# A graph network's relation sum: padding chunks left to GpSimd, the first dense tile transposed in place, and a tile's products put ahead of the next tile's transposes

## What is computed

```
seg = edge_type * n + dst
agg = segment_sum(x[src], seg, num_segments=34 * n)
cnt = segment_sum(ones, seg, num_segments=34 * n)
mean = agg.reshape(34, n, -1) / maximum(cnt, 1.0).reshape(34, n, 1)
h1 = einsum('rni,rio->no', mean, W_rel) + x @ W_root + b_rgcn
xw = h1 @ W_gcn
```

## Time and profile before

| | us |
|---|---|
| median of 3 timed runs | 2950.74 |
| lowest and highest | 2941.15 and 2956.47 |
| profiled execution | 2960.18 |
| its span, first to last instruction | 2958.1 |
| TensorE busy | 2565.2 (87%) |
| VectorE busy | 1549.8 (52%) |
| ScalarE busy | 1133.6 (38%) |
| GpSimd busy | 833.3 (28%) |

### The profile page before, as it was taken

One profiled execution on the slowest core, in us unless ns is written; L12 is line 12 of the kernel. 1 busy time (PEld: TensorE's weight loads), 2 busy tenths in 40 slices (PEclk: granted clock), 3 DMA queues, 4 the chain that ended last, 5 costly groups with the idle time before them and its releaser, 6 DMA issues.

```text
span 2958.1 us, 52403 instructions
## 1 busy us (share of the span) xinstructions
PE 2565.2 (87%) x14479; PEld 2416.0 (82%) x14513; DVE 1549.8 (52%) x2724; ACT 1133.6 (38%) x1977; POOL 833.3 (28%) x1090
## 2 busy tenths in 40 slices
PE   0666779859999999999999999678878889988799
PEld 0244579859999999999999999657778789978799
DVE  7754443463344434433444343488754687687634
ACT  3111242223444444444444444365532246446421
POOL 1677300004555555555555555100000000000000
PEclk9998889989999999999999999899989999989899
DMA  4100011144555555555555554687730200011102
GB/s 166 54 1 1 0 40 38 48 159 165 176 176 187 191 186 177 177 178 172 179 186 191 186 176 144 210 299 252 237 120 33 85 28 10 11 43 54 54 11 95
DMA packets 116745, 361.99 MB, mean 122 GB/s; under 512 B 22254, under 2 KB 22722, under 8 KB 116642
## 3 DMA queue, kind: packets, MB, share of 16 engines
q1 hardware_dynamic: 78241, 224.33, 22.0%
q0 software_dynamic: 38464, 137.17, 13.4%
HBM read 271.90 MB, written 93.37 MB: 123 GB/s over the span
## 4 chain that ended last, share of the span: by engine, by line
PE 77%; DVE 9%; issue 6%; ACT 3%; DMA 3%; DVEq 2%; ACTq 0%; SPq 0%; POOL 0%; POOLq 0%
PE ps L1352 51%; PE ps L1407 12%; PE ps L1343 5%; PE ps L1466 4%; PE ps L1541 3%; DMA land<-messages 1%; DVE h_act L999 1%; ACT land L750 1%; DVE w_a L924 1%; DVE land L1053 1%; DVEq L1184 1%; DMA land<-in_L_gnn_W 1%; ACT agg_w L760 1%; DVE land L1012 0%; DVE xw L1310 0%
## 5 line engine op out<-in xcount | busy, mean ns | idle before, releaser
L1352 PE MATMUL ps<-w_a,h_t 128*128 128x384 f32 x5580 | 1022.1, 339 | 1.9 <-DVE h_t L930 1.5
L1352 PEld LDWEIGHTS ps<-w_a,h_t 128*128 128x128 f32 x5580 | 971.5, 190 | 6.5 <-DVE h_t L930 3.9
L1407 PE MATMUL ps<-xw,agg_w 128*128 128x384 f32 x2800 | 528.6, 351 | 86.4 <-DVE agg_w L1024 55.3
L1407 PEld LDWEIGHTS ps<-xw,agg_w 128*128 128x128 f32 x2800 | 516.6, 198 | 95.3 <-issue 85.4
L1352 PE MATMUL ps<-xw,h_t 128*128 128x384 f32 x3132 | 577.3, 341 | 0.0
L1257 DVE TENSOR_TENSOR h_t<-ps,h_t 128x256 fp32r<-128x256 f32 x516 | 218.4, 423 | 678.4 <-ACT h_t L858 475.0
L1352 PEld LDWEIGHTS ps<-xw,h_t 128*128 128x128 f32 x3132 | 548.9, 188 | 0.0
L858 ACT ACTIVATE h_t<-ps 128x256 fp32r<-128x256 f32 x516 | 198.2, 384 | 669.5 <-PE ps L1352 443.3
L659 POOL DMA_INDIRECT messages<-land,rec_stage x172 | 199.6, 1161 | 353.0 <-ACT land L852 349.6
L1343 PE MATMUL ps<-ident,land 128*128 128x128 f32 x1398 | 196.8, 278 | 91.8 <-DVE land L937 33.3
L1343 PEld LDWEIGHTS ps<-ident,land 128*128 128x128 f32 x1398 | 168.8, 143 | 105.3 <-issue 44.8
(11 more groups left out here) (212 smaller groups left out, 2034.0 us busy)
## 6 DMA issues: line engine op xcount, KB each, us to landing
land<-in_L_gnn_W_rel SPq DMA_DIRECT2D x68, 1152.0 KB
land<-messages SPq DMA_DIRECT2D x92, 768.0 KB, 5.7
land<-x_state SPq DMA_DIRECT2D x40, 384.0 KB, 3.1
land<-in_L_gnn_W SPq DMA_DIRECT2D x10, 1152.0 KB
x_state<-land SPq DMA_DIRECT2D x30, 384.0 KB, 2.3
adj<-x_state SPq DMA_DIRECT2D x10, 384.0 KB, 3.0
h_act<-x_state SPq DMA_DIRECT2D x1, 3840.0 KB
h_table<-h_act SPq DMA_DIRECT2D x10, 384.0 KB, 2.3
```

The source lines that it names most:

```text
L1352: ins = pe.matmul(acc(h), h_t[:, a, k, :], w[:, b, k, h * HF:(h + 1) * HF], start=(k == 0 and a == 0 and b == 0), stop=(stop and k == KB - ...
L1407: ins = pe.matmul(ps[:, 2 + 2 * u + h, 0:wide], agg_w[:, a, b, :], xw[:, c, b, h * HF:h * HF + wide], start=first, stop=last, skip_group_c ...
```

## The change

Three parts. Padding chunks: `ctl_rel[NR]` is now the true number of chunks and `ctl_rel[NR + 1]` the rounded one plus 1. TensorE, VectorE and ScalarE's evacuations run to the true number. GpSimd's loop runs to the rounded number as before, with all its gathers and scatters; for the padding chunks ScalarE only passes its semaphore on, in a small loop (lines of `act.Fori(chunks, filled)`) whose last turn waits for a `ybuf` that GpSimd gives at the stage's end. First dense tile: TensorE transposes `h_act[:, 0]` itself, with no copy and no wait for `x_ring`'s return; VectorE gives `Q.ylow` before it waits for the bias row; it now waits for `R.stored` before it writes `rows[:, 2]`, and for `R.h_back` at the end of a tile's messages. Order: TensorE makes the products of tile t first, then the transposes of tile t + 1.

```diff
@@ GpSimd
-                                (R.wgot[2], 16, 16), (R.wgot[3], 16, 0), (R.copied, RING, 2)):
+                                (R.wgot[2], 16, 16), (R.wgot[3], 16, 0)):
                 pool.wait_ge(sm, fours * n + more)
                 pool.sem_inc(turn_taken, 1)
+            chunks = pool.value_load(ctl_rel[0:1, NR:NR + 1], min_val=1, max_val=CH)
+            pool.wait_ge(R.copied, chunks + 2)
+            pool.sem_inc(turn_taken, 1)
+            pool.sem_inc(R.ybuf, 1)
             pool.sem_inc(R.stored, 1)
@@ ScalarE
+            chunks, filled = bounds(act, ctl_rel, NR, CH + 1)
+            with act.Fori(chunks, filled) as c:
+                act.wait_ge(R.ybuf, c + 1)
+                act.sem_inc(R.yout, 1)
+
@@ VectorE, tables
-            dve.tensor_copy(ctl_rel[0:1, 1:NR], c_end[0:1, 0:NR - 1])
-            link(dve.tensor_scalar(ctl_rel[0:1, NR:NR + 1], half_f, float(RING), None, ALU.mult))
+            dve.tensor_copy(ctl_rel[0:1, 1:NR + 1], c_end[0:1, 0:NR])
+            link(dve.tensor_scalar(ctl_rel[0:1, NR + 1:NR + 2], half_f, float(RING), 1.0, ALU.mult, ALU.add))
@@ VectorE, sum
             dve.wait_ge(R.copied, chunks + 2)
-            dve.wait_ge(bias_land, 16 * (BIAS_ORDER.index("sum") + 1))
             dve.wait_ge(G["L0b"].act, NT)
             dve.sem_inc(Q.ofree, 2)
             dve.sem_inc(Q.ylow, LAND)
-            dve.wait_ge(R.h_back, 16)
-            dve.tensor_copy(rows[:, 2, :], tile_rows(h_act, 0)).then_inc(Q.copied, 1)
             turn_low(Q, 0)
+            dve.wait_ge(bias_land, 16 * (BIAS_ORDER.index("sum") + 1))
+            dve.wait_ge(R.stored, 1)
...
+                dve.wait_ge(R.h_back, 16)
                 if more:
                     turn_low(Q, t + 1)
@@ TensorE
-            pe.wait_ge(Q.copied, 1)
-            turn(Q, rows[:, 2, :])
+            turn(Q, h_act[:, 0, :])
 
             def sum_tile(t, more):
-                pe.wait_ge(Q.low, KG * t + KG)
-                if more:
-                    pe.wait_ge(Q.copied, t + 2)
-                    turn(Q, rows[:, 2, :])
                 pe.wait_ge(Q.ofree, t + 1)
                 for g in range(KG):
                     products(Q, t, g, w_a, rel_acc(t), False)
+                if more:
+                    pe.wait_ge(Q.copied, t + 1)
+                    turn(Q, rows[:, 2, :])
                 pe.sem_inc(turn_taken, 1)
```

## The result

| | before | after |
|---|---|---|
| median | 2952.05 us (4 runs, 2941.15 to 2956.47) | 2923.82 us (4 runs, 2921.26 to 2926.72) |
| profiled execution | 2960.18 | 2921.26 |
| its span | 2958.1 | 2919.2 |
| TensorE, VectorE, ScalarE, GpSimd busy | 2565.2, 1549.8, 1133.6, 833.3 | 2548.8, 1545.9, 1127.9, 830.2 |

The ratio is 0.991, with a 95% interval of 0.9881 to 0.9939. Later, on more runs beside each other, the same program gave 2936.48 against 2953.64 us, ratio 0.9934 (0.9908 to 0.9960). So the change makes the kernel 0.7 to 0.9% faster (0.4 to 1.2% by the intervals). The prediction said 2930, 21 us less than before; 28 and then 17 us were measured, with intervals that overlap.

A forecast was written before the change was run, and what follows sets the result against it. TensorE was taken as holding 77% of the chain of waits, with transfers bounding tile 0. Terms 3.05 + 1.0 + 4.47 = 8.5 us for tile 0, plus 12.5, made 21.0: 2950.74 to 2929.7 us, range 2918 to 2942.

The forecast's parts named there:

- `R.stored` 3.05 us earlier: End of relation stage: GpSimd's last scatter 3.37 us earlier, less 0.3 for an added register load.
- The new wait on ScalarE is harmless: Way into tile 0: high parts wait until 1875.1, yet TensorE is ready for messages 13 us earlier.
- Order of the first transfers: Start of tile 0's messages: pairs queued right behind `x_ring` land sooner; 1.0 taken of 0 to 3.5 us.
- rival 1: Ring order: first pair lands right behind `x_ring`, order term 3.5 instead of 1.0, 23.5 us won, 2927; chance 0.12.
- VectorE's stop in tile 0, 4.47 us: Tile 0: VectorE no longer stops four units ahead of TensorE, so the 7th pair's place frees 4.47 us sooner.
- Tiles 1 to 9, 12.5 us: Sum's tile boundaries: products ahead of transposes remove idle time; 12.5 us taken, between 8.8 and 14.1.
- TensorE now goes straight into the products: Sum's tile boundaries: TensorE's 14.5 us of idle time go, and VectorE's stop of 1.76 each too.
- At worst 8.8: Tiles 1 to 9: lower bound of the gain, nothing won where messages were late already (tiles 1, 2, 4).
- The median: Whole kernel: median of three timed runs, 2950.74 us, less 21.0 gives 2929.7.
- Rival 2: Tiles 1 to 4: message transfers set the pace and take the boundaries' gain; 8.5 us plus little remains, 2941; chance 0.12.
- Rival 3: End of relation stage: GpSimd's padding chunks wait for their landings, `R.stored` doesn't move, 18 us won, 2933; chance 0.12.
- Rival 4: Whole sum: TensorE's granted clock falls to 0.86, its work grows by 37 us, 2967, a loss; chance 0.06.

The follow-up runs named there:

- Experiment 4: The kernel before with only the padding chunks left to GpSimd alone, old order and old way into the sum kept; ratio to before 0.9983.
- experiment 6: The changed kernel with ScalarE's high parts of the first dense tile moved ahead of its loop for the padding chunks; ratio to before 0.9938.
- Experiments 8 and 9: Changed kernel, TensorE's tile loop written out: first with VectorE's copies dropped, ratio to before 0.9910; then with copies kept, single execution, 2931.03 us.
- experiment 3: The changed kernel with transposes ahead of products in the sum, as before; 2955.48 against 2962.40 us, ratio 0.9977.

## Why the prediction was right, and where its steps were off

The sum was 21.0 us; the touched stretch gave 18.8 to 20.0. It came this near partly by luck: between the first two profiles the way to tile 0's end gained 1.2 us more than forecast and tiles 1 to 9 gained 3.4 less. The absolute times that it named for the profile all came some 15 us early, since chunk 169's scatter stood at 1842.66 and not at 1857.58; counted from that scatter they can be compared. Its steps, in their order:

- **`R.stored` 3.05 us earlier**: 2.5. A padding chunk costs GpSimd 5.44 us and not 5.32 (the scatter waits 0.95 us behind its copy, not 0.84), and from the last weight gather to the bias row's issue it is 4.26 us instead of 3.62, so the added register load, with the waits and signals beside it, costs some 0.6, not 0.3. Experiment 4 shows the 2.5 alone.
- **The new wait on ScalarE is harmless**: right, and experiment 6 shows it. Products started 1.23 us after the bias row's issue (forecast 1.1). They took 8.38 us, not 9.7: the clock was at 0.50 from 1862 to 1864 and at 0.87 in the mean of the next 8 us, so it came back sooner after the first work than in the old passage. It made no difference, as TensorE was ready 3.5 us before the first message unit.
- **Order of the first transfers**: I took 1.0 of 0 to 3.5 us. The first conversion came 1.3 to 1.4 us nearer to the bias row's issue, but not by the order of the transfers, which was the same before. The prediction took the first conversion for the landing of the first pair. The rows of `x_ring`'s transfer and of GpSimd's relay of the four landings (issue to landing; first and last signal) in before, and the relay's in after:

```profile
h_act<-h_table SPq DMA_DIRECT2D x1, 1536.0 KB, 8.1
L674 POOLq EVENT_SEMAPHORE  x4: 17/17/17, 1888.6 to 1894.5; - x4
L376 ACTq TENSOR_LOAD <-ctl_quad x1: 273/273/273, 1889.9 to 1889.9; - x1
L678 POOLq EVENT_SEMAPHORE  x4: 17/17/17, 1871.8 to 1877.6; - x4
```

Before, `x_ring` landed at 1886.6, and the four pairs 2.0 us behind it and behind one another. ScalarE was late for the first: it made tile 0's high parts until 1889.2 and then loaded its loop's bounds (third row), so it began at 1890.91, 2.3 us after the landing, and worked the queue off without a gap. In after, the first pair again landed 1.9 us behind `x_ring` (1869.8), and ScalarE, with both jobs done by 1862.6, began 0.4 us later. That gives 1.9 us, of which `x_ring` took 0.6 back, as it landed 9.1 us after the bias row's issue instead of 8.5. So rival 1 was right that the queue is served in order, and the gapless conversions were no argument against it; but this order was already there, and there was nothing of it to win.

- **VectorE's stop in tile 0, 4.47 us**: gone. Tile 0 ended 103.3 (and 101.0) us after chunk 169's scatter before, 93.6 (and 93.1) after: 7.4 to 10.2 us, forecast 8.5. Less the two terms above, 5.8 us are left between the first two profiles and 4.1 between the second two, where 4.47 were forecast.
- **Tiles 1 to 9, 12.5 us**: 9.1 between the first two profiles (12.1 between the second two, where before had drops of the clock and TensorE was busy 3.0 us longer for it). This is the mis-sized term. The step that failed is "TensorE now goes straight into the products": at the loop's end it needs 0.45 us, the branch's 0.22 among them, which had lain under the 1.82 us of waiting; eight of them are 3.4 us. Experiments 8 and 9 show the cause. The bound passed to TensorE again, not to VectorE. Messages took back 1.9 us more, near the forecast's 1.6. "At worst 8.8" was just reached.
- **The median**: 28.2 us less in the first timing, 17.2 in the second. With 21 forecast and 19 to 20 in the stretch, the difference most likely lies in the counting stage, whose length varies by up to 24.6 us between profiles; only the profiled executions show their stages.

Rival 2 (transfers take it all) fell: the DMA engines were 82% busy in tiles 1 to 4, where over 90% was the sign against me. But it is next: of the 3.4 us that experiments 8 and 9 took from TensorE, 1.8 were kept in the one and nothing in the other, and the rest came back as waiting for messages. Rival 3 fell: stored moved. Rival 4, the clock, fell for the changed kernel: 0.94 in tile 0 and 1.00 from tile 1 on. But the clock does fall in this sum, in experiment 3's profile by enough to cost 6.9 us in tiles 1 to 3.

By the profiles the parts of the change don't add up: alone, the order gave 12 to 13 us of the stretch, the rest 1.7 to 2.5, together 19 to 20. The missing 4 to 6 us lie in experiment 3's low clock and later messages in tiles 1 to 3. That the new order protects against such falls is not shown: five of its ten profiles have some, though none with more than 7 us at the low level in tiles 1 to 9, where experiment 3's has 20. It is one profile, so it may also have been an unusual execution; the ratio of its twelve executions allows the parts to add up.

## What to carry to other kernels

A gap on the bounding engine hides small costs in front of it, here a loop's end of 0.45 us; take the gap out and the sum has to charge them, times the number of turns. When a transfer is moved ahead, move what tells of its landing with it: here a relay on a queue that was still busy held messages back 9.6 us (first conversion 21.6 against 12.0 us). And before a difference of two profiles is explained, cut both at the same events and profile the old kernel a second time: here 13 of 39 us were an untouched stage's own scatter. And a transfer's landing is read from the signal that tells of it, not from the first use of its data: here the reader itself was 2.3 us late, and the prediction built a term on it.

## What the runs showed of the hardware

- Executions of one program differed by 10.4 us in the counting stage, and fourteen profiles by 24.6 us (277.5 to 302.1 us), while the touched stretch agreed within 1 us in the repeats. The mean granted clock went with the stage's length, from 0.94 in the shortest to 0.88 in the longest; which of the two sets the other is open.
- TensorE's clock fell in the middle of the sum in profiles of both orders: a wait of 1.82 us behind 11.2 us of matmuls without a gap was once enough, and the same wait one tile earlier was not. In experiment 3's profile the low level cost 0.9 to 1.5 us of each of three tiles' products.
- The first four pairs, queued right behind `x_ring`, landed 1.9 to 2.0 us apart, one by one, in before and in after; asked for ahead of it, the first was ready 3.0 us sooner, and `x_ring` took 12.6 us to land instead of 8.7.
- A compare-and-branch of TensorE's loop took 0.22 us when taken and 0.08 when not, and with the register work beside it left TensorE idle 0.35 to 0.46 us.
